# A graph network on one Trainium2 core: 128 weight rows of the second relational layer composed by VectorE instead of TensorE

## What is computed

```python
def rgcn_gate_layer(x, row, col, edge_type, basis, att, gate_w, root, bias):
    w = jnp.einsum('rb,bio->rio', att, basis)      # 2 relations, 30 bases of 512x512
    x_j = x[col]
    for r in range(2):
        gate = jax.nn.sigmoid(x_j @ gate_w[r, :, 0])
        msgs.append(gate[:, None] * x_j @ w[r])
    msg = jnp.where((edge_type == 0)[:, None], msgs[0], msgs[1])
    agg = jax.ops.segment_sum(msg, row, num_segments=x.shape[0])
    return agg + x @ root + bias
```

## Time and profile before

| | |
|---|---|
| median of three runs | 501.38 us (500.28 to 502.05) |
| the profiled execution's own time | 502.33 us |
| its span | 500.5 us |
| TensorE busy | 469.4 us, 94% |
| VectorE busy | 296.0 us, 59% |
| ScalarE busy | 205.4 us, 41% |
| GpSimd busy | 105.5 us, 21% |
| mean granted TensorE clock | 0.987 |
| read from memory | 113.85 MB |

### The profile page before, as it was taken

The page is one execution under the profiler, slowest core; times in us unless marked ns, Lnnn a source line. Parts: engine busy times, 40 slices in busy tenths (PEclk is TensorE's granted clock), DMA queues, the critical chain, the costliest instruction groups (busy, mean ns, idle before and its releaser), DMA issues.

```text
span 500.5 us, 6858 instructions
## 1 busy us (share of the span) xinstructions
PE 469.4 (94%) x2310; PEld 316.4 (63%) x2310; DVE 296.0 (59%) x576; ACT 205.4 (41%) x368; POOL 105.5 (21%) x116
## 2 busy tenths in 40 slices
PE   7889987999979899899999999997899999999995
PEld 2334345666646566876756775674566688788884
DVE  5887797799778889565103579866123114542323
ACT  1788873456345443374126122674222004242000
POOL 0000287568766650000000240000000060000000
PEclk9999998899999999999999999999899999999998
DMA  8979678688878871999978799669987550200011
GB/s 252 428 270 411 208 209 272 192 265 258 278 246 269 269 239 45 412 341 379 372 302 296 317 326 359 241 289 369 381 339 283 204 169 1 85 1 1 22 43 42
DMA packets 29639, 121.21 MB, mean 242 GB/s; under 512 B 4330, under 2 KB 7354, under 8 KB 25246
## 3 DMA queue, kind: packets, MB, share of 16 engines
q1 hardware_dynamic: 17950, 92.33, 48.7%
q0 software_dynamic: 7856, 24.91, 16.1%
q10 hardware_dynamic: 3792, 3.43, 2.2%
HBM read 113.85 MB, written 6.82 MB: 241 GB/s over the span
## 4 chain that ended last, share of the span: by engine, by line
PE 66%; DMA 14%; DVE 12%; issue 4%; DVEq 2%; another core or an unknown queue 1%; ACT 0%; SPq 0%
PE ps L1446 13%; DMA basis<-in_basis 13%; PE ps L1501 12%; PE ps L1288 10%; PE ps L1539 9%; PE ps L1324 6%; DVE x L1000 3%; PE ps L1484 3%; PE ps L1372 3%; PE ps L1376 3%; PE ps L1373 2%; DVE rlo L1007 2%; PE ps L1254 1%; DVE X L935 1%
## 5 line engine op out<-in xcount | busy, mean ns | idle before, releaser
L1324 PE MATMUL ps<-xT_lo,xT_hi 128*128 128x512 f32 x237 | 62.6, 407 | 7.9 <-DVE x L1000 6.9
L1288 PE MATMUL ps<-basis,sel 128*32 128x512 f32 x496 | 59.0, 605 | 4.9 <-DMA basis<-in_basis 4.9
L609 POOL DMA_INDIRECT X<-u_rows,esrc x40 | 44.3, 1107 | 77.6 <-DMA u_rows<-X 56.8
L618 POOL DMA_DIRECT2D X<-w_layer x32 | 16.8, 653 | 206.8 <-DMA w_layer<-ev 206.8
L1324 PEld LDWEIGHTS ps<-xT_lo,xT_hi 128*128 128x128 f32 x237 | 42.9, 191 | 25.7 <-DVE x L1000 10.1
L609 POOL DMA_INDIRECT x_sb<-u_rows,esrc x39 | 43.3, 1110 | 18.5 <-issue 9.5
L1539 PE MATMUL ps<-Xr,CT_r 128*128 128x512 f32 x200 | 47.0, 389 | 0.0
L1539 PEld LDWEIGHTS ps<-Xr,CT_r 128*128 128x128 f32 x200 | 37.5, 188 | 7.8
L697 ACT ACTIVATE rhi<-x 128x512 fp32r<-128x512 f32 x60 | 35.5, 630 | 16.9 <-DVE x L1000 13.2
L1159 DVE SCALAR_TENSOR_TENSOR Xr<-ps,gate,Xr 128x512 fp32r<-128x512 f32 x20 | 14.9, 750 | 45.7 <-ACT Xr L796 45.7
L1007 DVE SCALAR_TENSOR_TENSOR rlo<-x,rhi 128x512 fp32r<-128x512 f32 x60 | 39.5, 687 | 0.0
(11 more groups left out here) (232 smaller groups left out, 810.9 us busy)
## 6 DMA issues: line engine op xcount, KB each, us to landing
basis<-in_basis SPq DMA_DIRECT2D x29, 2048.0 KB
X<-in_eaT SPq DMA_DIRECT2D x20, 256.0 KB
basis<-in_basis SPq DMA_DIRECT2D x8, 512.0 KB
X<-w_layer POOLq DMA_DIRECT2D x32, 128.0 KB, 3.0
w_layer<-ev SPq DMA_DIRECT2D x13, 256.0 KB, 10.6
X<-in_WhhT SPq DMA_DIRECT2D x3, 1024.0 KB, 14.9
basis_apart<-in_basis SPq DMA_DIRECT2D x1, 2048.0 KB, 19.0
X<-in_WihT SPq DMA_DIRECT2D x2, 1024.0 KB, 10.1
```

The costliest lines, as they stand in the source:

```text
L609: nc.gpsimd.indirect_dma_start(gat[e % GATHERS], None, t["u"][:, :], bass.IndirectOffsetOnAxis(ap=esrc[:, e:e + 1], axis=0)).then_inc(gat_ ...
L1288: mm = pe.matmul(bank[32 * g:32 * g + 32], sel[:, layer, s], held[:, g, s2], start=(s == 0), stop=(s == 3), tile_position=(0, 32 * g))
L1324: mm = pe.matmul(ps[:, EA_BANKS[s]], part[:, u % 2, s * P:(s + 1) * P], w, start=(i == 0), stop=(i == 2))
```

## The change

Tiles (1,6) and (1,7), the last 16 rows of each block of 64 in layer 1, are no longer composed by TensorE. These 128 rows form one contraction block, and VectorE adds them up: for each of 30 bases and 2 relations one operation on 128x512, `base * attention value + sum`. The first 14 bases come through GpSimd's queue into a ring of three places in `x_sb`, from when x1 is complete; the other 16 come through SyncE's queue into the two basis slots, after tile (1,5). The sums of the first 14 bases lie in the last two places of `x_sb`; from base 14 on they go to their place in the weights. `MIX_AFTER` says after which job how many of the 60 operations follow on VectorE.

The other three contraction blocks are then the first, second and third 16 rows of each 64. So everything that layer 1 contracts has to be in that order: ScalarE writes the ReLU's columns permuted, the root weights come by 16 DMAs, and the gate weights are first copied to an internal tensor in the new order. The composed rows have a new order in the stored tiles (relation outermost), and `load_w` needs 4 DMAs of 256 KB for a relation of layer 0 and 3 for one of layer 1, before 8 of 128 KB for both. The splits of layer 1's weights are over three blocks; the fourth is split by itself (`split_block`) and has a semaphore that TensorE waits for before each relation's first M of layer 1.

```diff
@@ -79,7 +79,19 @@
-W_AFTER_M = ((1, 1), (1, 4), (0, 3))
+TILES = (WT, WT - 2)
+LANES = 2 * ROWS
+BY_DVE = KT - 1
+RING_BASES = 14
+RINGS = 3
+SLOT_BASES = QTR * 2
+MIX_AFTER = {("M", 0, 0, 1): 2, ("M", 0, 1, 1): 2, ("M", 0, 2, 1): 2, ("M", 0, 3, 1): 2, ("M", 0, 4, 1): 2,
+             ("M", 0, 0, 0): 3, ("M", 0, 1, 0): 3, ("M", 0, 2, 0): 4, ("M", 0, 3, 0): 4, ("M", 0, 4, 0): 16,
+             ("out", 0, 0): 8, ("out", 0, 1): 7, ("out", 0, 2): 5}
+assert sum(MIX_AFTER.values()) == BASES * REL and RING_BASES + 2 * SLOT_BASES == BASES
+W_AFTER_M = ((1, 1), (1, 4))
+W_PARTS = (KT, 2 * KT - 1)
+BLOCK_SPLIT_AT = {("out", 0, 3): 1, ("out", 0, 4): 0}
 W_SPLIT_AT = {("z", 1): (0, 1), ("z", 3): (0, 0), ("out", 0, 2): (1, 1), ("out", 0, 3): (1, 0)}
@@ -96,7 +108,7 @@
-    composed = [("w", layer, tile) for layer in range(2) for tile in range(WT)][EARLY:]
+    composed = [("w", layer, tile) for layer in range(2) for tile in range(TILES[layer])][EARLY:]
     jobs = []
...
@@ -330,6 +343,13 @@
         h1 = x_sb
+        gate_lanes = [t["w"][1][0, r:r + 1, 1] for r in range(REL)]
+        ring = [x_sb[:, i] for i in range(RINGS)]
+        slot_bases = basis[:].rearrange("p a g s o -> p (a g s) o")
+        early_mix = [x_sb[:, RINGS + r] for r in range(REL)]
+        late_mix = [w_raw[:, r, KT - 1] for r in range(REL)]
...
@@ -446,6 +473,14 @@
+        def mix_rows(b):
+            return t["basis"][1][b].rearrange("(c q j) o -> q c j o", c=BLK, q=KT)[BY_DVE]
+        def lane_rows(at, order):
+            return at.rearrange(order, c=BLK, q=KT)
         def load_basis(eng, c):
@@ -497,6 +532,9 @@
                 load_basis(sp, c)
+            for r in range(REL):
+                sp.dma_start(gate_lanes[r].rearrange("a (q c j) -> a q c j", c=BLK, q=KT),
+                             t["gw"][1][:, r].rearrange("a (c q j) -> a q c j", c=BLK, q=KT)).then_inc(lanes_in, 16)
             sp.dma_start(W1bT, t["W1bT"]).then_inc(w1b_in, 16)
@@ -504,7 +542,7 @@
                 for r in range(REL):
-                    src = t["gw"][layer][:, r].rearrange("a (k n) -> a k n", k=KT)
+                    src = (t["gw"][0][:, r], gate_lanes[r])[layer].rearrange("a (k n) -> a k n", k=KT)
                     sp.dma_start(gate_rows[layer][r], src.broadcast_to([P, KT, P])).then_inc(gate_in[layer], 16)
@@ -558,7 +596,7 @@
                     for _ in range(2):
-                        if nb < 2 * WT * 2:
+                        if nb < 2 * (WT + TILES[1]):
                             load_basis(sp, nb)
@@ -568,6 +606,15 @@
                     sp.dma_start(t["w"][layer][tile][:, 0], ev[:, tile % 2]).then_inc(w_out[tile % 2], 16)
+                    if (layer, tile) == (1, TILES[1] - 1):
+                        for i in range(SLOTS):
+                            b = RING_BASES + i * SLOT_BASES
+                            if i == 0:
+                                sp.wait_ge(basis_used, WT + TILES[1])
+                            for j in range(SLOT_BASES):
+                                sp.dma_start(slot_bases[:, i * SLOT_BASES + j],
+                                             mix_rows(b + j)).then_inc(slot_in[i], 16)
                 if name == ("agg", KT - 1, 1):
@@ -583,11 +630,15 @@
                     sp.wait_ge(gate_sums, NT)
+                    sp.wait_ge(lanes_in, 16 * REL)
                     load_gate_rows(1)
                     full(sp, name)
-                    sp.dma_start(W2T[:], t["root"][1]).then_inc(root_in, 16)
+                    rows_of = t["root"][1].rearrange("(c q j) k o -> q k c j o", c=2, q=KT)
+                    for q in range(KT):
+                        for k in range(KT):
+                            sp.dma_start(W2T[2 * LANES * k:2 * LANES * (k + 1), q], rows_of[q, k]).then_inc(root_in, 16)
             for n in range(NT):
@@ -612,17 +663,28 @@
-                src = t["w"][layer].rearrange("w (g r k c s) h o -> r k c h (w g) s o", g=4, r=REL, k=KT, c=2)
-                for k in range(KT):
-                    for c in range(2):
-                        nc.gpsimd.dma_start(w_raw[64 * c:64 * c + 64, r, k], src[r, k, c, 0]).then_inc(w_in[r], 16)
+                src = t["w"][layer].rearrange("w (g s r c) h o -> r h c (w g s) o", s=2, r=REL, c=BLK)[r, 0]
+                if layer == 0:
+                    for k in range(KT):
+                        nc.gpsimd.dma_start(w_raw[:, r, k], src[2 * k:2 * k + 2]).then_inc(w_in[r], 16)
+                else:
+                    for q in range(BY_DVE):
+                        nc.gpsimd.dma_start(w_raw[:, r, q], src[:, q * LANES:(q + 1) * LANES]).then_inc(w_in[r], 16)
+            one_each = t["att"].rearrange("(b c) l r -> c l b r", c=QTR)
+            nc.gpsimd.dma_start(att_all[:], one_each[0:1, 1].broadcast_to([P, BASES, REL])).then_inc(att_all_in, 16)
             for layer in range(2):
                 for q in range(2):
-                    pool.wait_ge(w_out[q], 16 * (layer + 1) * WT // 2)
+                    pool.wait_ge(w_out[q], 16 * (WT + layer * TILES[1]) // 2)
                 full(pool, (("hn", NT - 1), ("M", 0, NT - 1, 0))[layer])
                     load_w(layer, r)
+                if layer == 0:
+                    pool.wait_ge(x1_ready, NT)
+                    for b in range(RING_BASES):
+                        if b >= RINGS:
+                            pool.wait_ge(mixed, REL * (b - RINGS + 1))
+                        nc.gpsimd.dma_start(ring[b % RINGS], mix_rows(b)).then_inc(ring_in[b % RINGS], 16)
@@ -672,7 +734,7 @@
                                     last = nc.scalar.activation(
-                                        sel[:, layer, 2 * group + s, 16 * r + s:16 * r + 16:2], maskc[:], ACT.Copy,
+                                        sel[:, layer, 2 * group + s, 16 * s + BLK * r:16 * s + BLK * (r + 1)], maskc[:], ACT.Copy,
                                         scale=att[:, group, layer, r:r + 1])
@@ -743,8 +805,14 @@
-                act.wait_ge(w_in[r], 16 * 2 * KT * (layer + 1))
-                nc.scalar.copy(w_hi[:, r], w_raw[:, r]).then_inc(w_hi_ready, 1)
+                act.wait_ge(w_in[r], 16 * W_PARTS[layer])
+                ks = slice(0, KT - layer)
+                nc.scalar.copy(w_hi[:, r, ks], w_raw[:, r, ks]).then_inc(w_hi_ready, 1)
+            def split_block(r):
+                act.wait_ge(mixed, BASES * REL)
+                nc.scalar.copy(w_hi[:, r, KT - 1], late_mix[r]).then_inc(block_hi_ready, 1)
@@ -765,7 +833,9 @@
                     elif kind == "out":
-                        ins = nc.scalar.activation(h1[:, name[2]], bank, ACT.Relu)
+                        act.wait_ge(mixed, REL * (RING_BASES + 1))
+                        ins = nc.scalar.activation(lane_rows(h1[:, name[2]], "p (q c j) -> p q c j"),
+                                                   lane_rows(bank, "p (c q j) -> p q c j"), ACT.Relu)
                     ins.then_inc(drained["A"], 1)
@@ -819,6 +889,8 @@
                     split_w(*W_SPLIT_AT[name])
+                if name in BLOCK_SPLIT_AT:
+                    split_block(BLOCK_SPLIT_AT[name])
                 if kind == "z":
@@ -834,7 +906,7 @@
-                    act.wait_ge(root_in, 16 * (name[1] + 1))
+                    act.wait_ge(root_in, 16 * (1, 1 + KT * KT)[name[1]])
                     nc.scalar.copy(root_hi, W2T[:]).then_inc(root_hi_ready, 1)
@@ -1094,7 +1166,43 @@
                 dve.wait_ge(w_hi_ready, 2 * layer + (2, 1)[r])
-                dve.tensor_tensor(w_lo[:, r], w_raw[:, r], w_hi[:, r].bitcast(F32), ALU.subtract).then_inc(w_ready, 1)
+                ks = slice(0, KT - layer)
+                dve.tensor_tensor(w_lo[:, r, ks], w_raw[:, r, ks], w_hi[:, r, ks].bitcast(F32), ALU.subtract
+                                  ).then_inc(w_ready, 1)
+            mixes = [0]
+            def mix_block(times):
+                for _ in range(times):
+                    n = mixes[0]
+                    mixes[0] += 1
+                    b, r = n // REL, 1 - n % REL
+                    if b < RING_BASES:
+                        dve.wait_ge(ring_in[b % RINGS], 16 * (b // RINGS + 1))
+                        rows_of, sums_of, into = ring[b % RINGS], early_mix[r], early_mix[r]
+                    else:
+                        i = b - RING_BASES
+                        dve.wait_ge(slot_in[i // SLOT_BASES], 16 * SLOT_BASES)
+                        rows_of, sums_of, into = slot_bases[:, i], late_mix[r], late_mix[r]
+                        if i == 0:
+                            full(dve, ("M", 0, NT - 1, 0))
+                            sums_of = early_mix[r]
+                    if n >= REL:
+                        dve.wait_ge(mixed, n - REL + 1)
+                    if b == 0:
+                        dve.wait_ge(att_all_in, 16)
+                        ins = dve.tensor_scalar(into, rows_of, att_all[:, b, r:r + 1], None, ALU.mult)
+                    else:
```

(12 more changed lines are left out.)

8 lines of the change are left out of this document (added).

## The result

| | before | after |
|---|---|---|
| median of four runs, same chip | 501.72 us (500.28 to 503.41) | 523.66 us (517.73 to 526.78) |
| ratio | 1 | **1.0397** (1.0293 to 1.0501) |
| the profiled execution, its span | 502.33, 500.5 us | 526.78, 525.0 us |
| granted clock, mean | 0.987 | 0.961 |

The change costs 4%; 498.4 us was forecast. Executions of one kernel differ with the granted clock: the ratios in this document leave out those that are more than 1.5% above the kernel's fastest, the medians and ranges don't, and the profiles shown of the kernel after and of flat (run 6) are of such slower executions.

What follows compares the result with a forecast made beforehand. Bound by TensorE's own work and, at one point, tile (1,4)'s arrival. -7.6 + 1.2 + 1.8 + 1.6 = -3.0 us takes the profiled 502.33 to 499.3; being 0.95 above the median, 498.4 was predicted, range 495.0 to 502.0.

Steps and rivals of the forecast that it cites:

- What is added in DMA: Step costing the new ring, slot, root, stored-weight and table transfers: +1.8 us at tile (1,4), 0 for the rest.
- +1.8 us for tile (1,4): First three ring loads share the DMA engines with arriving tile (1,4) and delay it: +1.8 us, bounds 0 and 2.1.
- The stored weights: Second layer's stored weights, loaded some 14 us earlier by 6 issues instead of 16: 0.
- The ring: Ring loads during VectorE's sums: hold them up only if one comes every 3.7 us; half-size loads landed after 3.0.
- The root in 16 pieces: Second root matrix, requested after the last output tile, read five products, 14 us, later: 0.
- VectorE's sums: 60 sums at 0.61 us, 36.6 in all, margins 2.3 at the fifth drain, 3.8 at layer 1's first product.
- thin cover: Rival: VectorE's sums go at 0.72 us or ring loads come late; 499.5 to 502.5 us, typically 500.1; chance 0.16.
- The slower rival: VectorE bounds the output tiles; loss beyond 0.3% at 0.78 us a sum, or ring loads only every 3.7; chance 0.12.
- The table: Attention values in 8-byte runs on GpSimd's queue, early, while DMA engines are 9% busy from 186 to 197: 0.
- Removing the compose jobs: Tiles (1,6) and (1,7) leave TensorE, 4.02 and 3.57 us, both on the path: -7.6 us.
- second clock loss: TensorE's clock drops after the grown gap before M(0,3,1): +1.6 us, bounds 0 and 3.0.
- The two sums ahead of the low part: Two sums delay the low part of x's transpose: +1.2 us, gap before M(0,3,1) from 1.45 to some 2.7.

Runs made afterwards that it cites:

- flat (run 6): All loads recut (as run 4), plus layer 1's gate weights laid out in the new order so VectorE's gate sums read flat rows: 506.74 us, 1.0057.
- run 1: Kernel after, with layer 0's stored weights loaded by 16 DMAs of 64 partitions instead of 8 of 128: 504.31 us, 1.0243.
- run 7: flat (run 6) without 11 of the 14 ring loads, all 60 sums kept, output not the reference's: 498.29 us, 0.9918.
- run 2: Kernel after, with the attention table loaded as 128 runs of 240 bytes instead of 3840 of 8 bytes: 509.96 us, 1.0352.
- run 3: Kernel after, rows reordered so sources of ring, slot, layer 1 weight and root loads begin with 16, root in 4 DMAs: 503.72 us, 1.0233.
- run 4: Kernel after with the edits of run 1, run 2 and run 3 together: 496.77 us, 1.0124.
- paced: flat (run 6) with the 16 slot loads held back, eight until 14 sums are done and eight until 24: 1.0032.
- shift: flat (run 6) with five sums moved from in front of M(0,4,0)'s drain to behind it: 1.0085.
- both: flat (run 6) with slot loads held back, fewer sums before M(0,4,0)'s drain and none ahead of the low part of x's transpose: 1.0038.
- run 10: both with ScalarE and TensorE orders mended, slot loads at sums 12 and 22: 1.0057; the same without 11 ring loads, output not the reference's: 0.9825.
- last: run 10's full-load kernel, slot and ring bases alternating after nine, root-weight split ahead of two sums, slot loads at sums 11 and 20: 492.74 us, 1.0009.

## Why the prediction was wrong

**The step that failed is "What is added in DMA".** All of it was costed at 0 except +1.8 us for tile (1,4), as if any transfer could use all engines and land as fast as in a quiet stretch. In its place the runs showed some 7 us for layer 0's weights (run 1) and, for the ring, gaps of TensorE of 11.35 and 6.71 us, of which some 7 us in the whole time are left when all loads have 16 or more in front (run 7 against flat):

- *The stored weights, "6 issues instead of 16: 0".* The text speaks of layer 1 alone; that layer 0's loads changed their form too stands in the change, and I gave it no term. They landed after 28.7 us in place of 14.3. With their old form M(0,0,1) came 6.7 us earlier (run 1 against run 2, 328.93 and 335.60, on one chip), level with the kernel before, and the ratio fell from 1.040 to 1.024.
- *The ring.* I took it to be safe unless a load came only every 3.7 us, "the loads of half the size landed 3.0 us after issue, and three are under way at a time". That 3.0 is the median over both layers; the loads that run among basis tiles, as the ring's do, took 14.3. The ring's took 9.2 (median) and up to 19.1 us. With three under way that is one every 3.1 us, inside the bound of 3.7, and VectorE waited all the same, so the bound was the wrong test. Two different waits came of it. The first three were issued together at 354.08, while the DMA engines were full (share 1.00 from 354 to 375 us). VectorE stood before each of them, and the third holds up the low part before M(0,3,1):

```profile
354.08 1.78 POOL L687 DMA_DIRECT2D x_sb<-in_basis x3 [60.45 <-DVE x L1148]
```
```profile
361.19 0.88 DVE L1195 TENSOR_SCALAR x_sb<-x_sb,att_all 128x512 f32<-128x512 f32 x2 [4.20 <-DMA x_sb<-in_basis]
...
366.14 1.42 DVE L1197 SCALAR_TENSOR_TENSOR x_sb<-x_sb,att_all 128x512 f32<-128x512 f32 x2 [3.41 <-DMA x_sb<-in_basis]
...
374.34 1.41 DVE L1197 SCALAR_TENSOR_TENSOR x_sb<-x_sb,att_all 128x512 f32<-128x512 f32 x2 [6.12 <-DMA x_sb<-in_basis]
375.67 1.28 DVE L1273 TENSOR_TENSOR xT_lo<-ps,xT_hi 128x512 fp32r<-128x512 f32 x2
```

  The second wait is the round trip of a refill. A place is asked for only after its own two sums, so where the sums stand behind a drain that waits for TensorE, the next load starts late too: GpSimd issued ring loads at 354, 362, 368, 376, 385 and 388 us. The twelfth was issued at 404.85 and its sums began at 413.09, ahead of M(0,4,0)'s drain, the gap of 6.71 us. With 16 in front the first kind shrank to the forecast 2.7 us at M(0,3,1) (run 3); the second stayed at 3.5 to 5.9 us (runs 3, 4, 6 and paced) and went only with the loads (run 7) or moved elsewhere (shift, both and run 10).
- *The root in 16 pieces, "14 us, later: 0".* SyncE needed 14.56 us to issue them, 0.91 each, where four loads with 16 in front took 2.52 in run 3, 0.63 each, and ScalarE waited 4.4 us. For the 16 slot loads it needed 27.13, against 11.53 in run 3. The trace shows no wait of TensorE for them: here the margin was large enough. SyncE's issues in the kernel after:

```profile
389.12 27.13 SPq L616 DMA_DIRECT2D basis<-in_basis x16
449.54 14.56 SPq L641 DMA_DIRECT2D W2T<-in_root x16
```


**VectorE's sums.** Pitch 0.67 us, forecast 0.61: ten took 6.71 in one piece.

```profile
422.55 6.71 DVE L1197 SCALAR_TENSOR_TENSOR X<-basis,att_all,X 128x512 f32<-128x512 f32 x10
```

The row that I took (0.61) multiplies by a constant; the added form takes its scalar from memory, one for each partition, and stood in the earlier trace rows as the drain: 0.75 us, the next operation after 0.66. That the scalar makes the difference wasn't tested by itself. Over 50 sums this is 3 us, and takes most of the 3.8 us of margin; the rival "thin cover" had the mechanism, and the margins of 2.3 and 3.8 us were too small to be called free. The slower rival asked for a dearer sum (0.78 us), which never came: sums kept 744 to 749 ns with and without the loads beside them (runs 6 and 7). Its second clause, the ring load "only every 3.7 us", is the one that came true in kind, and I had put 0.12 on the two together.

**The table.** Here the prediction was right: it had the table pass between 186 and 200 us, and it was issued at 186.6 and landed 8.0 us later (kernel after, 180 to 200 us).

```profile
att_all<-in_att POOLq DMA_DIRECT2D x1, 30.0 KB, 8.0
```

The many small packets that GpSimd's queue q0 moves with layer 0's weights are easily taken for the table, but they belong to the weights. Run 2, with the table in runs of 240 bytes, has them too; run 1, with the table of 8-byte runs and the weights in the old form, doesn't (q0 from 274 to 320 us of run 2, then of run 1: packets, MB, share):

```profile
q0 software_dynamic: 4224, 2.13, 23.9%
```
```profile
q0 software_dynamic: 768, 2.10, 15.5%
```

**What held.** Removing the compose jobs gives what was summed: with the ring's data there, the sum of -3.0 us is -0.6%, and run 7 measured -0.8% and run 10 -1.75%. Their traces have no second clock loss, and run 10's has no sums ahead of the low part, so by the same terms they should be at -4.6 us (-0.9%) and -5.8 us (-1.2%). Both lie inside the measured intervals (-0.5 to -1.2% and -1.2 to -2.3%), which are too wide to confirm single terms. The two sums ahead of the low part make the gap before M(0,3,1) 2.77 us (forecast 2.7) in runs 3, 4, 6 and 7. Tile (1,4)'s gap grew from 2.72 to between 3.09 and 3.6, once to 4.11 (run 2), and not to 4.5, so the +1.8 was mostly under half true. The second clock loss (+1.6) came in run 4 and in paced and shift (2.04 or 2.05 us for four matmuls) and not in runs 3, 6 and 7, behind the same gap of 2.77 or 2.78 us. The Trainium skill ("TensorE: Matmul & The Clock Gate", What's actually happening) says that the gate follows how busy the engine has lately been, on a beat that isn't tied to the kernel. The prediction concluded that one and the same gap may or may not drop the clock; these runs agree.

**Still open.** The number of engines that serve one of layer 0's loads wasn't seen by itself, nor was the first dimension changed there without the number and size of the loads. And whether a fourth ring place or a ring that doesn't share its engines with the slot loads would turn last into a gain wasn't tried.
